# A convolution on two engines: channels split 128 to 64 instead of 96 to 96, taps paired on TensorE, and the output product one image later

## The reference, cut to what matters

```
h = layernorm(x, n1_g, n1_b) @ w_in + b_in           # 96 -> 192 channels
p = depthwise_conv_3x3(h, k_conv)                    # zero padding, 9 taps for each channel
q = p + scans of p along rows and columns            # a fixed linear map over the 256 tokens
x = x + (layernorm(q) * on_g + on_b) @ w_out + b_out # 192 -> 96 channels
x = x + mlp(layernorm(x, n2_g, n2_b))                # the next stage
```

## Time and profile before

| | us |
|---|---|
| median of three runs | 1340.66 (1339.4 to 1341.65) |
| the profiled execution | 1337.15 |
| its span, first to last instruction | 1335.4 |
| mean granted TensorE clock, as a share of full speed | 0.949 |
| TensorE / VectorE / ScalarE / GpSimd busy in the span | 1167.9 / 741.0 / 509.8 / 391.1 |
| first work of the stage / last copy of its output | 261.4 / 434.5 |

### The profile page before, as it was taken

The page is one execution under the profiler, slowest core; times in us unless marked ns, Lnnn a source line. Parts: engine busy times, 40 slices in busy tenths (PEclk is TensorE's granted clock), DMA queues, the critical chain, the costliest instruction groups (busy, mean ns, idle before and its releaser), DMA issues. The chain is left out here.

```text
span 1335.4 us, 24086 instructions
## 1 busy us (share of the span) xinstructions
PE 1167.9 (87%) x8929; PEld 804.4 (60%) x8929; DVE 741.0 (55%) x2104; ACT 509.8 (38%) x823; POOL 391.1 (29%) x590
## 2 busy tenths in 40 slices
PE   0699998799997879999999998689888978999998
PEld 0266665467776556666766666457455544577776
DVE  1568873357775335666666667466555565332322
ACT  0166652233332224333333332254343422355543
POOL 1366646334342631011010110415200000353522
PEclk9899998989998899999999999799799999799999
DMA  5320000000000000000000000000000000000000
GB/s 69 68 54 2 2 2 1 0 1 0 0 0 0 1 0 1 1 1 1 1 1 1 1 1 1 1 1 1 1 2 1 1 2 1 1 7 13 7 13 13
DMA packets 27300, 9.21 MB, mean 7 GB/s; under 512 B 25345, under 2 KB 27200, under 8 KB 27200
## 3 DMA queue, kind: packets, MB, share of 16 engines
q1 hardware_dynamic: 24720, 7.13, 2.9%
q10 hardware_dynamic: 2480, 0.73, 0.4%
HBM read 6.27 MB, written 1.57 MB: 6 GB/s over the span
## 5 line engine op out<-in xcount | busy, mean ns | idle before, releaser
L150 POOL TENSOR_TENSOR ln_v<-MV,eps 128x2 f32<-128x2 f32 (+3 forms) x81 | 15.9, 197 | 439.9 <-PE bank L1075 246.2
L1137 ACT ACTIVATE fa_e<-bank 128x1024 f32<-128x1024 f32 x64 | 65.6, 1025 | 159.0 <-PE bank L1045 159.0
L1940 PEld LDWEIGHTS bank<-e_w,ex_G 128*128 128x128 f32 x768 | 90.6, 192 | 14.4 <-issue 14.1
L2055 DVE SCALAR_TENSOR_TENSOR X<-bank,ex_L,X 128x96 f32<-128x96 f32 x128 | 31.7, 309 | 114.2 <-PE bank L1940 108.4
L1189 DVE TENSOR_REDUCE fa_z<-bank 128x4 f32<-128x1024 f32 x64 | 78.3, 1224 | 25.2 <-PE bank L1027 23.4
L1932 PE MATMUL bank<-hT,e_w 96*128 96x512 f32 x192 | 91.5, 614 | 0.0
L1940 PE MATMUL bank<-e_w,ex_G 128*128 128x96 f32 x768 | 90.0, 274 | 0.0
L1983 ACT ACTIVATE ex_G<-bank,e_b 128x512 f32<-128x512 f32 x96 | 64.5, 689 | 61.8 <-PE bank L1932 59.1
L1787 DVE TENSOR_REDUCE ca_z<-bank 128x2 f32<-128x256 f32 x96 | 48.8, 550 | 49.9 <-PE bank L1514 49.9
L1045 PE MATMUL bank<-fa_a,fa_b 64*128 64x256 f32 x512 | 73.5, 406 | 1.1 <-DVE fa_a L1196 1.1
L153 POOL TENSOR_TENSOR ln_r<-ln_v,minus_half 128x2 f32<-128x2 f32 (+3 forms) x81 | 71.6, 884 | 0.0
(11 more groups left out here) (251 smaller groups left out, 2624.5 us busy)
## 6 DMA issues: line engine op xcount, KB each, us to landing
X<-in_x SPq DMA_DIRECT2D x16, 96.0 KB
out_tokens<-X SPq DMA_DIRECT2D x8, 192.0 KB, 2.2
e_w<-in_L_ffn_w SPq DMA_DIRECT2D x2, 576.0 KB
bias0r<-in_L_conv_rpb_table ACTq DMA_DIRECT2D x16, 24.0 KB
m0w<-in_L_conv_mlp_w SPq DMA_DIRECT2D x2, 144.0 KB
m1w<-in_L_conv_w SPq DMA_DIRECT2D x2, 144.0 KB
f_w<-in_L_ffn_W SPq DMA_DIRECT2D x2, 142.5 KB
mixer<-in_mixer SPq DMA_DIRECT2D x1, 256.0 KB
```

The costliest lines, as they stand in the source:

```text
L1137: act.activation(E[v % 2][:], k.banks[:, b:b + 2, :].rearrange("p i (c q) -> p i c q", c=2), ACT.Exp).then_inc(s["exp"], 1)
L1940: last = pe.matmul(bank[4 + e % 2][:, t * C:(t + 1) * C], G[e % 2][:, j, t * P:(t + 1) * P], k.ew2[:, e, j, :], start=(j == 0), stop=(j == ...
```

## The change

VectorE now convolves 128 channels (all partitions) and TensorE the other 64. Those 64 are held twice in `grid`, in partitions 0 to 63 and, moved by one column, in 64 to 127; a product over 128 rows then sums two taps of a row, and a third of `diag` holds the single ones. Six products remain, and even and odd ones write different partitions of the bank, so that a pair can run side by side; `stack2` adds the two sums when they are transposed. ScalarE writes `grid` in three pieces. The mixer's result moves to a bank of its own, and bank 4 takes the result of three `keep_warm` products an image. Each loop is written out. TensorE's round n becomes: warm, tokens(n+1), out(n-2), mix(n-1), taps(n), widen(n+1), warm, back(n-1), warm, conv_t(n). VectorE does residual(n-2) after tap 4, norm2(n-1) after tap 5, norm2b(n-1) after tap 7. GpSimd normalises two images ahead, and releases the first before it clears `grid` and fills `diag`.

```diff
--- before.py
+++ after.py
...
+def in_turn(steps, body):
+    for n in range(steps):
+        body(n, n % 2, n == 0, n == steps - 1)
 def keep_warm(pe, k, out, times=1):
...
-    k.win = weight("w_in", [C, CI], a["L1_conv_w_in"])
-    k.bin = weight("b_in", [C, 2], a["L1_conv_b_in"].rearrange("(j p) -> p j", p=C))
-    k.kconv = sb("k_conv", [C, 2, 9])
-    for j in range(2):
-        loads.append((k.kconv[:, j, :], a["L1_conv_k_conv"].rearrange("a b o (j p) -> j p (a b o)", p=C)[j]))
-    k.ong = weight("on_g", [C, 2], a["L1_conv_on_g"].rearrange("(j p) -> p j", p=C))
-    k.onb = weight("on_b", [C, 2], a["L1_conv_on_b"].rearrange("(j p) -> p j", p=C))
-    k.wout = weight("w_out", [C, 2, C], a["L1_conv_w_out"].rearrange("(j p) c -> p j c", p=C))
+    k.win = sb("w_in", [C, 2 * P])
+    loads.append((k.win[:, 0:CI], a["L1_conv_w_in"]))
+    loads.append((k.win[:, CI:2 * P], a["L1_conv_w_in"][:, P:CI]))
+    k.bin, k.ong, k.onb = sb("b_in", [P, 2]), sb("on_g", [P, 2]), sb("on_b", [P, 2])
+    k.kconv, k.wout = sb("k_conv", [P, 2, 9]), sb("w_out", [P, 2, C])
+    k.stack2 = weight("stack2", [P, CI - P], a["stack2"])
+    for j, p0, channels in ((0, 0, slice(0, P)), (1, 0, slice(P, CI)), (1, CI - P, slice(P, CI))):
+        rows = slice(p0, p0 + channels.stop - channels.start)
+        for t, name in ((k.bin, "b_in"), (k.ong, "on_g"), (k.onb, "on_b")):
+            loads.append((t[rows, j:j + 1], a["L1_conv_" + name][channels, None]))
+        loads.append((k.kconv[rows, j, :], a["L1_conv_k_conv"].rearrange("a b o p -> p (a b o)")[channels]))
+        loads.append((k.wout[rows, j, :], a["L1_conv_w_out"][channels]))
...
+        NARROW = CI - P
+        part = (P, NARROW)
...
-        acc = [sb(f"acc{i}", [C, TOK]) for i in range(2)]
-        acc1 = sb("accb", [C, TOK])
-        diag = sb("diag", [P, 9, C])
+        acc = [sb(f"acc{i}", [P, TOK]) for i in range(2)]
+        acc1 = sb("accb", [P, TOK])
+        diag = sb("diag", [P, 6, NARROW])
...
-        ZT = sb("zT", [C, 2, 2, P])
+        ZT = sb("zT", [P, 2, 2, P])
...
             @block.gpsimd
...
-                pool.memset(diag[:], 0.0)
+                def norm(n, slot):
+                    normalise(pool, k, s, n, 2, k.Y[slot][:, 0:2, :], k.bout, n - 1)
+                norm(0, 0)
...
-                for tap in range(9):
-                    last = pool.tensor_scalar(diag[0:C, tap, :], k.ident[0:C, 0:C], k.kconv[:, 1, tap:tap + 1], 0.0, ALU.mult, ALU.add)
-                last.then_inc(s["diag"], 1)
+                low, high = slice(0, NARROW), slice(NARROW, P)
+                column = k.kconv[:, 1, :].rearrange("p (y x) -> p x y", x=3)
+                for i in range(2):
+                    pool.tensor_tensor(diag[low, 3 * i:3 * i + 3, :], k.stack2[low, None, :].broadcast_to([NARROW, 3, NARROW]),
+                                       column[low, 2 * i, :, None].broadcast_to([NARROW, 3, NARROW]), ALU.mult).then_inc(s["diag"], 1)
+                pool.tensor_tensor(diag[high, 0:3, :], k.stack2[high, None, :].broadcast_to([NARROW, 3, NARROW]),
+                                   column[high, 1, :, None].broadcast_to([NARROW, 3, NARROW]), ALU.mult).then_inc(s["diag"], 1)
+                pool.memset(diag[high, 3:6, :], 0.0).then_inc(s["diag"], 1)
+                pool.wait_ge(s["diag"], 4)
...
                 def rstd2(n):
...
-                def norm(n, slot):
-                    normalise(pool, k, s, n, 2, k.Y[slot][:, 0:2, :], k.bout, n - 1)
-                norm(0, 0)
-                def body(n, slot, first, last):
-                    if not last:
-                        norm(n + 1, 1 - slot)
-                    if not first:
+                norm(1, 1)
+                for n in range(IMAGES + 1):
+                    if n + 2 < IMAGES:
+                        norm(n + 2, n % 2)
+                    if n >= 1:
...
-                pipeline(pool, IMAGES, body)
...
-                rstd2(IMAGES - 1)
...
             @block.tensor
...
-                            last = pe.matmul(bank[4][:, t * CI:(t + 1) * CI], k.mixer[:, j, t * P:(t + 1) * P], loc[:, j, :],
+                            last = pe.matmul(bank[7][:, t * CI:(t + 1) * CI], k.mixer[:, j, t * P:(t + 1) * P], loc[:, j, :],
...
                 def back(n):
+                    keep_warm(pe, k, bank[4][:])
...
-                            last = pe.transpose(bank[5][0:C, (2 * j + t) * P:(2 * j + t + 1) * P], Z[:, t, j * C:(j + 1) * C], k.ident[:])
+                            last = pe.transpose(bank[5][0:part[j], (2 * j + t) * P:(2 * j + t + 1) * P], Z[:, t, j * P:j * P + part[j]], k.ident[:])
...
                 def out(n):
...
-                            last = pe.matmul(o, ZT[:, j, t, :], k.wout[:, j, :], start=False, stop=(j == 1))
+                            last = pe.matmul(o, ZT[0:part[j], j, t, :], k.wout[0:part[j], j, :], start=False, stop=(j == 1))
...
                 def tokens(n, slot):
...
-                        last = pe.matmul(bank[1][0:C, j * TOK:(j + 1) * TOK], k.win[:, j * C:(j + 1) * C], k.hT[slot][:, 0:TOK], start=True, stop=True)
+                        last = pe.matmul(bank[1][:, j * TOK:(j + 1) * TOK], k.win[:, j * P:(j + 1) * P], k.hT[slot][:, 0:TOK], start=True, stop=True)
...
-                def taps(n, slot, first):
+                def taps(n, slot):
...
-                    for tap in range(9):
-                        if tap == 2 and not first:
-                            mix(n - 1)
-                        y, x = divmod(tap, 3)
-                        last = pe.matmul(bank[3][0:C, 0:TOK], diag[:, tap, :], grid[slot][:, 1, y:y + SIDE, x:x + SIDE],
-                                         start=(tap == 0), stop=(tap == 8))
+                    for i in range(6):
+                        y, single = i % 3, i // 3
+                        last = pe.matmul(bank[3][64 * (i % 2):64 * (i % 2) + 64, 0:TOK], diag[:, i, :],
+                                         grid[slot][:, 1, y:y + SIDE, 2 * single:2 * single + SIDE],
+                                         start=(i < 2), stop=(i > 3), skip_group_check=True)
...
                 def conv_t(n, slot):
...
+                    keep_warm(pe, k, bank[4][:])
...
-                    for half, src in ((0, acc[slot]), (1, acc1)):
-                        for j in range(2):
-                            last = pe.transpose(bank[2][:, (2 * j + half) * C:(2 * j + half + 1) * C], src[:, j * P:(j + 1) * P], k.ident[0:C, 0:C])
+                    for t in range(2):
+                        tok = slice(t * P, (t + 1) * P)
+                        pe.transpose(bank[2][:, t * CI:t * CI + P], acc[slot][:, tok], k.ident[:])
+                        last = pe.matmul(bank[2][:, t * CI + P:(t + 1) * CI], acc1[:, tok], k.stack2[:], start=True, stop=True)
...
-                pe.wait_ge(s["diag"], 1)
-                def body(n, slot, first, last):
-                    if not last:
+                pe.wait_ge(s["diag"], 4)
+                for n in range(IMAGES + 2):
+                    slot = n % 2
+                    keep_warm(pe, k, bank[4][:])
+                    if n + 1 < IMAGES:
...
-                    taps(n, slot, first)
-                    if not first:
+                    if n >= 2:
+                        out(n - 2)
+                    if 1 <= n <= IMAGES:
+                        mix(n - 1)
+                    if n < IMAGES:
+                        taps(n, slot)
+                    if n + 1 < IMAGES:
+                        widen(n + 1, 1 - slot)
+                    if 1 <= n <= IMAGES:
...
-                    if not last:
-                        widen(n + 1, 1 - slot)
-                    if not first:
-                        out(n - 1)
-                    conv_t(n, slot)
-                pipeline(pe, IMAGES, body)
-                mix(IMAGES - 1)
-                back(IMAGES - 1)
-                out(IMAGES - 1)
+                    if n < IMAGES:
+                        conv_t(n, slot)
...
             @block.scalar
...
-                        last = act.activation(ZT[:, j, :, :], bank[5][0:C, j * 2 * P:(j + 1) * 2 * P].rearrange("p (t q) -> p t q", t=2),
-                                              ACT.Identity, bias=k.onb[:, j:j + 1], scale=k.ong[:, j:j + 1])
+                        n_rows = part[j]
+                        last = act.activation(ZT[0:n_rows, j, :, :], bank[5][0:n_rows, j * 2 * P:(j + 1) * 2 * P].rearrange("p (t q) -> p t q", t=2),
+                                              ACT.Identity, bias=k.onb[0:n_rows, j:j + 1], scale=k.ong[0:n_rows, j:j + 1])
...
                 def tokens(n, slot):
...
-                    for j in range(2):
-                        last = act.activation(grid[slot][0:C, j, 1:1 + SIDE, 1:1 + SIDE],
-                                              bank[1][0:C, j * TOK:(j + 1) * TOK].rearrange("p (i c) -> p i c", c=SIDE),
-                                              ACT.Identity, bias=k.bin[:, j:j + 1])
```

(46 more changed lines are left out.)

## The result

The changed kernel took 1326.88 us (median of six runs, 1324.14 to 1330.75), against 1340.03 us (1334.52 to 1343.11) for six runs of the kernel before: a ratio of 0.9904, with a 95% interval of 0.9881 to 0.9927. The profiled execution took 1325.31 us (span 1323.4), 11.84 less than that of before. 1326.3 was forecast.

A forecast was written before the change was run, and what follows sets the result against it. The bound was a dependency loop through the engines' queues, 9.55 us an image, not TensorE alone; images -8.1, start -4.3, end -2.0 sum to -14.4, median 1340.66 to 1326.3 us; range 1318 to 1347, first case alone 1321 to 1331.

The forecast's parts named there:

- The circle: Convolution stage, z to next z through all engines' queues: 9.556 us an image becomes 8.98, -8.1 us over 14 images.
- The output product to the copy of `X`: Step from TensorE's output product to VectorE's copy of its result: 1.75 us, taken from the kernel before.
- the sum stays: Tiling-mode changes on TensorE, even at 0.6 us more an image, fit its spare time and leave the forecast unchanged.
- the residual to tap 5: VectorE's step from the copy of `X` to the next tap: 1.48 us.
- tap 5: VectorE's tap between residual and statistics: 0.52 us, a third of 1.57 for three taps.
- the output product started: Step from ScalarE's `cm_zT` to TensorE's output product: 1.17 us.
- TensorE's share: TensorE's work an image: 7.15 us against 8.42 before, so TensorE leaves the bound by 2 us.
- Rival (a), the falling clock: TensorE's clock falls in its idle gap, 1.5 us an affected image: some images 1331 to 1340 (0.20), most 1341 to 1348 (0.31).
- Rival (b), VectorE as the bound: VectorE's own work sets the image at 7.93 us; stage gains 22.8 us, kernel 1311.6 us; chance 0.04.
- Rival (c): TensorE's paired products don't run side by side: +1.13 us an image there, kernel 1326 to 1328 us; chance 0.07.
- Start: Stage start to first z: tap 0 at 267.2, z at 279.4 against 283.74, -4.3 us.
- End: Fifteenth z to last copy of `X`: -3.7 us at full clock, taken as -2.0 for a lower clock.

The follow-up runs named there:

- full_rows: The changed kernel with the output product's second half padded with zeros from 64 to 128 rows: 1315.17 us, ratio 0.9808 to the kernel before.
- three_taps: The changed kernel with VectorE's statistics one tap earlier, so three taps stand before z: 1322.69 us, ratio 0.9872 to the kernel before.
- full_three: The changed kernel with both the zero-padded output product and the statistics one tap earlier: 1307.5 us, ratio 0.9756 to the kernel before.
- serial_pairs: The changed kernel with its six products reordered 0, 2, 4, 1, 3, 5: 1329.25 us, ratio 0.9921 to the kernel before.
- order_only: The kernel before with the new queue order, loops written out and mixer's own bank; 96 and 96 channels, nine products, no warming: 1334.12 us, ratio 0.9935.
- split_only: The changed kernel's channel split and paired products in the old order within an image, new GpSimd start, no warming: 1357.48 us, ratio 1.0134 to the kernel before.
- no_warm: The changed kernel without its three warming products an image: 1333.49 us (ten runs), ratio 0.9953 to the kernel before.
- full_three_cold: The changed kernel with zero-padded output product and statistics one tap earlier, without warming products: 1309.68 us, ratio 0.9784 to the kernel before.

## Why the prediction was right, point by point

**The circle** was the right one: 8.98 forecast, 8.99 read and 9.007 in the mean, -7.7 for -8.1 us; the stage gave 14.95 for 14.4. Three experiments moved it by making single terms smaller (`full_rows`, `three_taps`, `full_three`), and `serial_pairs`, with 0.5 more on TensorE, did not move it.

**But its terms were off both ways, and the sum was partly luck.** The output product to the copy of `X` took 2.12 where the sum had 1.75. Three changes of rows lie in this stretch and add 0.51 to the 1.61 that it takes without them (`full_rows`). The sum took it from before, 128 and 96 rows alike, and weighed changes of mode only as TensorE's room ("the sum stays"). That is the step that failed: the product lies on the circle, and its price is paid fourteen times. Against it the residual to tap 5 took 1.33 for 1.48, tap 5 0.39 for 0.52, and the output product started 0.11 sooner than 1.17; together 0.39, which covers the 0.37 (the other steps were 0.03 longer). Tap 5 I had priced as a third of three that each read the sum of the one in front; statistics don't read it and start 0.39 behind it. The residual is 1.33 in `order_only` and in `split_only` too, so it comes from what both have of the change beside order and split, of which the loops written out are the likely part; no run has them alone. The 1.75 of before against 1.61 in `full_rows` is as open.

The Trainium skill, TensorEngine Tiling (Array Packing), section Key Properties, says that TensorE drains when the tiling mode changes. By that rule the four changes around the 64-row products had to cost something, and the traces agree: 2.01 us with four, 1.68 with two, 1.41 with none.

**TensorE's share** was 8.06 and not 7.15 (and the terms of the kernel before add up to 8.47, not 8.42): output product +0.61, mixer 1.49 for 1.30, widening 0.97 for 0.86. The taps were right at 1.44. Between full products the mixer takes 1.32 (`order_only`), in front of the paired taps 1.42 (`full_rows`), and with a 64-row product ahead too 1.50; so the pairs cost 0.1 on each side. By this wrong term the wait was 0.92 in one piece, not 1.8; whether the clock needed that is not shown.

**Rival (a), the falling clock**, did not come in the change, and is real without the warming: 0.89 in the mean, 9.80 us an image in the profile, stage 171.96 against 172.78 before. It struck nine images there, for 0.1 to 1.1 us in six and 2.3 to 2.5 in three, 1.3 in the mean, where the prediction's price was 1.5. The prediction gave the warming products no part in holding the clock; by `no_warm` they matter here: the six executions of the change had mean clocks of 0.945 to 0.952, and seven of ten without warming 0.934 to 0.944. What decides between a clock that holds and one that falls stays open: the traces of `split_only`, idle 37 of 144 us, and `full_three_cold`, idle 19 of 113, stood at 1.00, and that of `no_warm`, idle 19 of 137, did not.

**Rival (b), VectorE as the bound**, is reached, or met, by the two edits: 8.10 with no wait shown, against the 7.93 forecast, with the circle at 8.09 beside it. A tap on 128 partitions costs 517 ns in the mean against 515 on 96, as taken. **Rival (c)**: the pairs run side by side, 1.44 us for the six. Half by half they took 0.48 more and it did not matter; the full 1.13 would have been more than TensorE's wait of 0.92.

**Start** gave 5.3 for 4.3 us: tap 0 was 4.0 sooner, as worked out, and from tap 0 to the first z it took 11.3, where 12.2 was taken. **End** gave 2.0, as forecast, with the clock at 0.56 behind the last z.

**Order or split?** Neither alone gives the images' gain. Gains against the kernel before, in the traces:

| us | start to first z | fourteen images | fifteenth z to last copy of `X` | stage |
|---|---|---|---|---|
| order alone | 1.53 | 1.49 | 3.12 | 6.14 |
| split alone, with the new start of GpSimd | 5.89 | -9.97 | -2.82 | -6.90 |
| both, with warming | 5.31 | 7.68 | 1.96 | 14.95 |

## What to carry to other kernels

Follow one item around all queues, including an engine whose queue order alone ties two steps, and price each edit by whether it lies on that circle: reducing TensorE's products for the taps from nine to six paired ones, 3.87 to 1.44 us an image, gave a loss (ratio 1.0134) until the order was changed. A product with fewer rows isn't cheaper: where it alternates with full ones, pad it with zeros (ratio 0.9808 against 0.9904). When a wait appears right in front of a value's consumer, look for work of the same engine that can be moved into it (the third tap: 0.22 us an image).

## What the runs showed of the hardware that was not expected

- A change between 128-row and 64-row products on TensorE costs about 0.17 us at full clock (0.35 for two, 0.68 for four, the mixer's 0.08 with them), and one between full products and pairs of 64 columns about 0.1 (the widening is busy for 1.13 behind the pairs and 1.03 behind transposes in `split_only`).
- Six products of 64 columns, ordered so that no two neighbours but one write different halves, took 1.92 us, 0.32 each, where 0.43 each was expected from the 96-column ones; in pairs they took 1.44. Whether they still overlap in part or are shorter by themselves was not tried.
- The clock stood at 1.00 over 113 us with TensorE waiting 0.93 for z and 0.32 for `cm_zT` in an image (`full_three_cold`), and over 144 us with a wait of 2.41 for z in each image (the trace of `split_only`). It fell in `no_warm`, where the first image had waits of 1.53 and 0.32 ahead of the fall and later ones 1.14 and 0.32. The length of the waits alone doesn't sort these cases, and the same kernel fell in some executions and not in others.
